# Attention scores as 64-row products of two heads at once, with a head pair and a query tile as the unit of work

## The reference, cut to what matters

```python
k = keys @ Wk.T + bk;  gk = key_grid @ Wgk.T + bgk        # 256 + 256 keys
v = values @ Wv.T + bv; gv = key_grid @ Wgv.T + bgv
q = (queries @ Wq.T + bq)                                 # of the layer-normalised x
att = einsum('bhqd,bhdk->bhqk', q, k_new) / 8             # 16 heads, 64 long
att_k = where(attention_mask, -inf, att[..., :256])       # first 256 keys only
att = softmax(concat([att_k, att[..., 256:]]))
out = einsum('bhqk,bhkd->bhqd', att, v_new) @ Wo.T + bo
x = x + out
x = x + fp8_gemm(layernorm(x), ffn_kernel) + ffn_bias
```

## Time and profile before

| | before |
|---|---|
| median of 3 runs | 2909.78 us (2906.48 to 2913.43) |
| span of the profiled execution | 2906.8 us |
| PE busy | 2793.8 us, 96% |
| PE weight loads busy | 2431.0 us, 84% |
| DVE busy | 2315.1 us, 80% |
| ACT busy | 1982.3 us, 68% |
| POOL busy | 2099.0 us, 72% |
| mean granted TensorE clock | 0.995 of full |

### The profile page before, as it was taken

One profiled execution on the slowest core, in us unless ns is written; L12 is line 12 of the kernel. 1 busy time (PEld: TensorE's weight loads), 2 busy tenths in 40 slices (PEclk: granted clock), 3 DMA queues, 4 the chain that ended last, 5 costly groups with the idle time before them and its releaser, 6 DMA issues.

```text
span 2906.8 us, 68146 instructions
## 1 busy us (share of the span) xinstructions
PE 2793.8 (96%) x20352; PEld 2431.0 (84%) x20352; DVE 2315.1 (80%) x3793; ACT 1982.3 (68%) x4742; POOL 2099.0 (72%) x2504
## 2 busy tenths in 40 slices
PE   5999999999999999999999999999999999999997
PEld 4888888888888888888888888888888888888886
DVE  5888778888778887788887788877888877888776
ACT  4666676766677666767666776667676667766674
POOL 4777777777768777777777687777777776877775
PEclk9999999999999999999999999999999999999998
DMA  5333333333333333333343333333333433333331
GB/s 170 82 77 90 76 86 82 80 79 91 72 90 87 76 90 76 87 83 79 79 92 71 90 87 76 90 77 86 85 79 78 93 69 90 87 76 90 78 82 37
DMA packets 176029, 243.02 MB, mean 84 GB/s; under 512 B 25472, under 2 KB 92544, under 8 KB 176000
## 3 DMA queue, kind: packets, MB, share of 16 engines
q1 hardware_dynamic: 176000, 242.66, 35.6%
HBM read 66.40 MB, written 8.39 MB: 26 GB/s over the span
## 4 chain that ended last, share of the span: by engine, by line
PE 61%; DVE 17%; issue 13%; ACT 7%; DMA 1%; DVEq 1%; POOL 0%; SPq 0%; ACTq 0%; POOLq 0%
PE ps_misc L555 20%; PE ps_o L658 10%; PE ps_pt L645 10%; PE ps_misc L599 8%; PE ps_scores L631 5%; PE ps_scores L632 5%; DVE pt_lo L941 5%; DVE kv_out L912 3%; PE ps_scores L634 2%; ACT probs L786 2%; DVE q_lo L889 2%; DVE scr_b L875 1%; DVE o_t L949 1%; ACT zq_out L751 1%; DVE scr_a L877 1%
## 5 line engine op out<-in xcount | busy, mean ns | idle before, releaser
L481 POOL TENSOR_SCALAR probs<-probs,recips 128x512 f32<-128x512 f32 x1024 | 698.4, 694 | 457.0 <-DVE recips L936 456.8
L795 ACT CAST pt_hi<-ps_pt 128x512 fp32r<-128x512 f32 x1024 | 551.7, 595 | 319.8 <-PE ps_pt L645 314.5
L786 ACT ACTIVATE probs<-ps_scores,neg_max 128x512 f32<-128x512 f32 x1024 | 696.0, 688 | 23.5 <-DVE neg_max L932 11.4
L941 DVE TENSOR_TENSOR pt_lo<-ps_pt,pt_hi 128x512 fp32r<-128x512 f32 x1024 | 655.2, 680 | 53.2 <-ACT pt_hi L795 50.3
L932 DVE TENSOR_REDUCE neg_max<-ps_scores 128x2 f32<-128x1024 f32 x512 | 621.1, 1213 | 9.5 <-PE ps_scores L634 9.5
L658 PE MATMUL ps_o<-pt_hi,v_hl 128*128 128x256 f32 x2048 | 554.6, 302 | 1.0 <-DVE o_t L949 1.0
L645 PE MATMUL ps_pt<-ident,probs 128*128 128x128 f32 x4096 | 531.5, 273 | 1.6 <-DVE pt_lo L941 1.6
L658 PE MATMUL ps_o<-pt_lo,v_hl 128*128 128x256 f32 x2048 | 511.4, 281 | 0.0
L645 PEld LDWEIGHTS ps_pt<-ident,probs 128*128 128x128 f32 x4096 | 464.5, 141 | 8.6 <-POOL probs L481 2.0
L631 PE MATMUL ps_scores<-k_hl,q_hh 128*128 128x512 f32 x1024 | 456.8, 446 | 9.0 <-issue 4.7
L632 PE MATMUL ps_scores<-k_hl,q_lo 128*128 128x512 f32 x1024 | 407.1, 398 | 0.0
(11 more groups left out here) (106 smaller groups left out, 6567.1 us busy)
## 6 DMA issues: line engine op xcount, KB each, us to landing
k_hl<-k_split SPq DMA_DIRECT2D x1024, 128.0 KB, 2.3
mask_sb<-mask_dram SPq DMA_DIRECT2D x128, 256.0 KB, 3.3
q_hh<-q_hh SPq DMA_DIRECT2D x256, 128.0 KB, 2.4
x_sb<-x_dram SPq DMA_DIRECT2D x32, 256.0 KB, 2.8
side_raw<-side_t_dram SPq DMA_DIRECT2D x32, 256.0 KB, 3.6
scr_b<-ctx_t_dram SPq DMA_DIRECT2D x32, 256.0 KB, 2.8
out_dram<-y SPq DMA_DIRECT2D x32, 256.0 KB, 2.1
probs<-wq_t_dram SPq DMA_DIRECT2D x1, 1024.0 KB, 5.1
```

The source lines that it names most:

```text
L481: nc.gpsimd.tensor_scalar(probs[:, h % 2, t, :], probs[:, h % 2, t, :], recips[:, h % 2, t:t + 1], 1.0, ALU.mult, ALU.mult).then_inc(norm_ ...
L786: nc.scalar.activation(probs[:, h % 2, t, :], ps_scores[:, h % 2, t, :], ACT.Exp, bias=neg_max[:, h % 2, t:t + 1], scale=-1.0, accum_out=s ...
L795: nc.scalar.copy(pt_hi[:, h % 2, 2 * k:2 * k + 2, :], ps_pt[:, k, :, :]).then_inc(pthi_done, 1)
L941: V.tensor_tensor(pt_lo[:, h % 2, 2 * k:2 * k + 2, :], ps_pt[:, k, :, :], pt_hi[:, h % 2, 2 * k:2 * k + 2, :].bitcast(F32), ALU.subtract). ...
```

## The change

**Scores.** q and k are kept where the chunk leaves them: `q_hi`, `q_lo`, `k_hi`, `k_lo` hold two heads, one on partitions 0 to 63, the other on 64 to 127. Each of the three products hi·hi, lo·hi, hi·lo is issued with 64 rows, for the first head on the upper half of the array's rows and right behind it for the second head on the lower half; they go to different PSUM banks. The program gives these products an array position of row 0 or row 64 and a size of 64 by 128; all others have position 0 and 128 by 128. The two mask products follow with 128 rows, as before.

**Unit of work.** A unit u is a head pair and one query tile (`pair, t = u // 2, u % 2`). It has as many scores, exponentials, transposes and casts as a head had; the two entries of `ps_scores`, `probs` and `ps_pt` are now two heads of one tile instead of two tiles of one head (in `ps_pt`: instead of two halves of the keys). A head's output product needs both units of its pair. `outputs` of head h-2 now stands ahead of `transposes` of unit h, and `pt_hi` and `pt_lo` have three buffers instead of two.

**Removed.** `k_split`, `place_keys`, `place_queries`, their semaphores and waits, the zeroing of half of `q_lo`, and `B_EARLY`. The split of q is one operation on 128 partitions on each of ACT and DVE instead of two on 64. GpSimd writes k_hi and k_lo directly to their place.

**Chunks.** `PLACES` has the same chunks at other places; in the opening part k1 comes ahead of v0.

Of the diff, cut to its core:

```diff
 PLACES = {
-    (0, "A"): ("k0", 1), (0, "B"): ("q", 1), (1, "A"): ("wo0_prev", 0), (1, "B"): ("k1", 1),
+    (0, "A"): ("k0", 1), (0, "B"): ("q", 1), (1, "A"): ("k1", 1), (2, "A"): ("wo0_prev", 0), (2, "B"): ("v0", 1),
...
-B_EARLY = (1, 2)
...
+def pt_turn(pair, e):
+    return 0 if e == 0 else 1 + pair % 2
...
-            hh = q_hh[:, n % 2].rearrange("p (a e) s -> p e a s", e=2)
-            ql = q_lo[:, n % 2].rearrange("p (a e) s -> p e a s", e=2)
-            src = zq_out[:].rearrange("p (a s) -> p a s", s=S)
-            owns = [slice(e * DK, (e + 1) * DK) for e in range(2)]
-            return [(hh[own, e], ql[own, e], src[own]) for e, own in enumerate(owns)]
+            flat = "p a s -> p (a s)"
+            return [(q_hi[:, n % 2].rearrange(flat), q_lo[:, n % 2].rearrange(flat), zq_out[:])]
...
-                        sp.dma_start(k_hl[to, n % 2, 2 * int(kind[1]) + e, :].bitcast(F32),
-                                     k_split[own, part, :].bitcast(F32)).then_inc(k_placed, 16)
...
-                    sp.dma_start(hh[other, e], hh[own, e]).then_inc(q_placed, 16)
...
-            def scores(h, g, free=True):
+            def scores(u, g, free=True):
+                pair, t = u // 2, u % 2
+                r, a = pair // 2 % 2, pair % 2
+                rows = slice(t * P, (t + 1) * P)
+                if free:
+                    pe.wait_ge(exp_done, 2 * (g - 1))
+                for n, (q, k) in enumerate(((q_hi, k_hi), (q_lo, k_hi), (q_hi, k_lo))):
+                    for e in range(2):
+                        own = slice(e * DK, (e + 1) * DK)
+                        mm(ps_scores[:, u % 2, e, :], q[own, r, a, rows], k[own, r, a, :],
+                           start=(n == 0), stop=False)
+                for e in range(2):
+                    row = (2 * a + e) * QT + t
+                    m = mask_sb[:, r, row * S:(row + 1) * S].bitcast(FP8E5)
+                    last = mm(ps_scores[:, u % 2, e, 0:S], mask_weight[:], m, start=False, stop=True)
+                last.then_inc(scores_done, 1)
+
+            def transposes(u, g, first=False):
+                for e in range(2):
+                    pe.wait_ge(norm_done, 2 * g + e + 1)
+                    if not first:
+                        pe.wait_ge(ptlo_done, 2 * g - 1 + e)
...
+            def outputs(h, g, first=False):
+                pair, e = h // 2, h % 2
+                pe.wait_ge(ptlo_done, 2 * g + (2 if e else 3))
...
                     do((h, "A"))
+                    if not (first and h < 2):
...
+                        outputs((h - 2) % H, g - 2, first and h == 2)
                     transposes(h, g, first and h == 0)
...
+                    do((h, "B"))
```

More of the change, by code:

```diff
@@ L83, in kept @@
             return False
-        return not (last and (kind == "zt_next" or place[0] > LAST_OWN))
+        own = kind in PREV or group > 0
+        return own or not last
     return {place: PLACES[place] for place in SLOT_ORDER if place in PLACES and kept(place, PLACES[place])}
@@ L384, in batch @@
             def batch(b, first=False, last=False):
-                c = Chunks(b, first, last)
                 for h in range(H):
@@ L408, in batch @@
                         load_mask(b + 1, 0)
-                    for place in ((h, "A"), (h, "B")):
-                        kind, n = c.at.get(place, ("", 0))
-                        if kind in K_KINDS:
-                            place_keys(kind, n, c.before(place, KV) + 1)
-                        if kind == "q":
-                            place_queries(n, c.before(place, ZQ) + 1)
             batch(0, first=True)
@@ L470, in split_chunk @@
                 wait_apart(pool, "pool", misc_free, copied)
-                if kind in K_KINDS and not (isinstance(k_before, int) and k_before == 0):
-                    wait_apart(pool, "pool", k_placed, K_PLACES * k_before)
                 nc.gpsimd.tensor_scalar(hi, src, 1.0, 0.0, ALU.mult, ALU.add).then_inc(kv_hi_part, 1)
@@ L503, in _ @@
             for j, (kind, n) in enumerate(PROLOGUE[2:]):
-                split_chunk(kind, n, j + 3, j, sum(k in K_KINDS for k, _ in PROLOGUE[2:2 + j]))
+                split_chunk(kind, n, j + 3, j)
             def batch(b, first=False, last=False):
@@ L519, in batch @@
                         norm(h + 1, H * b + h + 1)
-                    if h == 3 and not first:
+                    if h == 4 and not first:
                         rstd_of(0, mv_y, var_y, rstd_y, b)
@@ L524, in batch @@
                         copy_x(b)
-                    if h == 4 and not first:
+                    if h == 5 and not first:
                         scale_quant_in(b - 1)
@@ L637, in transposes @@
-            def transposes(h, g, first=False):
-                pe.wait_ge(norm_done, QT * (g + 1))
-                for k in range(2):
-                    if not first:
-                        pe.wait_ge(ptlo_done, 2 * g - 1 + k)
-                    for j in range(2):
-                        for t in range(QT):
-                            kt = 2 * k + j
-                            last = nc.tensor.transpose(ps_pt[:, k, j, t * P:(t + 1) * P],
-                                                       probs[:, h % 2, t, kt * P:(kt + 1) * P], ident[:])
-                    last.then_inc(pt_full, 1)
@@ L649, in outputs @@
-            def outputs(h, g, first=False, tiles=range(KT)):
-                if 0 in tiles:
-                    pe.wait_ge(ptlo_done, 2 * (g + 1))
-                    if not first:
-                        pe.wait_ge(o_done, g)
-                n, i = h // GH, h % GH
-                for kt in tiles:
+            def scores(u, g, free=True):
[14 more added lines that the diff above has]
+                last.then_inc(scores_done, 1)
@@ L657, in outputs @@
+            def outputs(h, g, first=False):
+                pair, e = h // 2, h % 2
+                pe.wait_ge(ptlo_done, 2 * g + (2 if e else 3))
+                if not first:
+                    pe.wait_ge(o_done, g)
+                n, i = h // GH, h % GH
+                for kt in range(KT):
                     for pt in (pt_hi, pt_lo):
-                        last = mm(ps_o[:, 0:S], v_hl[:, n % 2, kt, i, :], pt[:, h % 2, kt, :],
+                        last = mm(ps_o[:, 0:S], v_hl[:, n % 2, kt, i, :], pt[:, pt_turn(pair, e), kt, :],
@@ L727, in _ @@
             batch(B - 1, last=True)
+            outputs(H - 2, H * B - 2)
             outputs(H - 1, H * B - 1)
@@ L1047, in batch @@
                         quantise_weights(h - 4)
-                    if h in (5, 6) and not first:
-                        quantise(b, h - 5)
+                    if h in (6, 7) and not first:
+                        quantise(b, h - 6)
                     if h == 7 and not last:
```

185 lines of the change are left out of this document (71 added, 114 removed), and 10 rows, old and new, of the table PLACES.

## The result

The changed kernel takes 3012.98 us (median of 4 runs, 3009.55 to 3014.7) against 2908.53 of the kernel before: a ratio of 1.0356, with a 95% interval of 1.0341 to 1.0371. It is 104 us slower. 2850 us were forecast, with a range of 2790 to 3050: the result lies inside the range, but on the other side of the kernel before.

The account below looks back on a forecast made before the run. TensorE was taken as the bound, hardly ever kept waiting. Scores gave 59 us less, everything else 0: 2906.8 - 59 = 2848, plus 3 from span to median, 2851, rounded 2850 us; own range 2820 to 2895, full range 2790 to 3050.

Parts of the forecast that it names:

- What bounds the kernel: Whole kernel before: TensorE is hardly ever kept waiting, so the time is the sum of distances between its starts.
- The scores, after: Scores of a unit: three pairs side by side, lag, two masks and entry sum to 1.075 us; 59 us less in all.
- I take the middle, 0.04: Entry to a unit's first 64-row product: 0.04 us, between 0 and 0.08 seen at changes of kind on the full array.
- The lag of 0.10: Scores: the second product of each pair starts one load behind the first, seen once a unit, 0.10 us.
- its 1.19: Scores of a head before the change: 1.19 us, over 512 heads 609 us, 21% of the span.
- Rival 1: Scores block edges: every array-size change runs the array dry, up to 0.16 us each; 3035, half price 2970; chance 0.24.
- rival 3: Scores pairs: a half's weights can't load while it streams, so further pairs take 0.335 instead of 0.235; 2953; chance 0.09.
- So no new wait: 0: Outputs and transposes: only their order changes, and the split of the transposes stays covered; 0, or 16 us if cover fails.
- the prediction's own sign: Scores block in the profile after: if the time moves and its length doesn't, the prediction's whole reasoning is wrong.
- Copies and splits: DMA copies and q splits on ACT and DVE: copies were hidden, worth 0 to 3 us; splits 0.

Follow-up runs that it names:

- e6_before_late: The kernel before, with the statistics, scaling and quantisation of y one step later and xq_prev at (8, B) instead of (7, B): 2960.5 us (1.0175).
- e3_one_half: The changed kernel with both products of every pair on rows 0 to 63, so the two can't run side by side: 3253.6 us (1.1184).
- e5_mask_between: The changed kernel with xq_prev at (9, A) instead of (8, B) and both masks moved between the first and second pair: 3143.6 us (1.0813).
- e18_fine2: The changed kernel with other places, y's quantisation two operations each in steps 5 to 7, next x's statistics and normalisation one step later: 2910.3 us (1.0009).
- e7_two_units: The changed kernel with xq_prev at (9, A) and both units' scores of a head pair in one block every odd step: 3407.8 us (1.1749).

## Why the prediction was wrong

**What bounds the kernel**: right for the kernel before, and too quickly carried over. TensorE was the bound only as long as DVE's results just arrived. e6_before_late shows how close that was: one step later costs 52 us.

**The scores, after**: the halves do run together (0.23 from pair to pair; e3_one_half costs 241 us more). The terms mis-sized were the edges. "I take the middle, 0.04" for the entry is 0.09, the exit, for which I had nothing, is 0.10, and in the block shown the masks take 0.28 instead of 0.23 (ahead of outputs the median is 0.23). The lag of 0.10 has the right size by luck: no second product starts a load behind the first (0.49 alone, 0.50 for both); it is the load of the first pair, which nothing hides behind a change of size, so it is a part of the edge. The row became 12 us shorter at full clock, not 59: 47 us of the miss. The reasoning by the nearest rows, changes of kind on the full array, had no change of size among them, and the middle between 0 and 0.08 was no estimate of it. The sum also took its 1.19 from a block behind outputs, where one between two chunks has 1.27.

**Rival 1** had the place, ahead of the first 64-row product and of the first mask; measured is about 0.1 an edge (0.28 for two edges and the load in e5_mask_between). That takes the gain but, at +4 us over all blocks, is no loss. Its direction came true, but for the most part by waits that it did not name, and its 2970 for half the price doesn't follow from the sum, which gives 1.235 to 1.275 us a unit and so 2933 to 2953. The Trainium skill's page "TensorEngine Tiling (Array Packing)", Key Properties, says that a change of mode drains TensorE; the trace agrees in so far as each way in and out costs 0.28 us. On rival 3 the trace disagrees with Part 3 of the Trainium skill's "TensorE: Matmul & The Clock Gate": third pairs follow 0.23 behind second ones, and their loads begin as the second pair does (1405.89), so loads run beside products of the same half.

**Outputs, transposes and chunks: "So no new wait: 0"** is the step that failed. It covers 115 of the 163 us by which I missed: 81 of idle time and 34 of half clock behind it. By the prediction's own sign (the time moves, the block's length doesn't) it was wrong in its whole reasoning; that 3013 us lies in its range is owed to the width that rivals 1 and 3 gave it. I followed one chain (`pt_lo`) and k's way over GpSimd, and not the third that the new table touches: `ps_misc` is freed by DVE behind `pt_lo`, and where v stands at B and another chunk at A of the next step, only a block of scores lies between. Nor did I see that `normalise_y`, the quantisation and xq moved by a step while the moments and the normalisation of the next x stayed, which puts them side by side on DVE. The kernel before already showed this as its longest wait, `ps_misc` behind `kv_out`. The runs show it as a matter of places: with other places and smaller pieces (e18_fine2) most of the idle time (115 us, against 99 before) and all of the additional half clock (0.995) are gone, and the scores are the same.

**Copies and splits**: right, they were hidden. The splits gave DVE and ACT time back that neither needed; q_lo takes 894 ns on 128 partitions, between my 0.69 and 1.65 (zt_lo, which gave the 1.65, has 0.82 in the changed kernel):
```profile
L847 DVE TENSOR_TENSOR q_lo<-zq_out,q_hi 128x512 fp32r<-128x512 f32 x128 | 114.5, 894 | 73.1 <-ACT q_hi L736 73.1
```

What stays open: how much of the 52 us of e6_before_late is the place of xq and how much the rest of the shift; what the new order of outputs and transposes costs by itself, which no run separates from the places; how far the kernel before could be tuned in the same way; and whether fewer changes of size would pay, since the one arrangement tried (e7_two_units) broke the chain behind the scores.

## What to carry to other kernels

Two half-height products side by side take the time of one, but here each way into and out of the half-height size cost 0.28 us; so count what lies between two changes. Three pairs in place of four full-height products save 0.235 us, which was too little to gain. When a rewrite comes with a new order, price the order by itself: follow each buffer with one copy (here `ps_misc`) to the engine that frees it, and to what stands ahead of that copy in its queue. An engine that is 73% busy can hold one that is 94% busy if its work comes in lumps.

## What the runs showed of the hardware

- Products of 64 rows on different halves of the array, into different PSUM banks, run together at the pace of one: 0.23 us for a pair of 512 columns, with a load for each (e3_one_half: 0.46 for two on the same half). The two start within 0.01 us, and their loads within 0.01 too (two loads in 0.19 us).
- A change from 128 rows to 64 delays the next product by 0.09, the change back by 0.10. Behind the change to 64 rows the first product's weight load isn't hidden, another 0.10, with a partner or without one (e3_one_half). Together 0.28 us (e5_mask_between: 142 us for 512).
- Idle gaps of TensorE of 1.10 and 0.98 us, 2.6 us apart, came ahead of a fall to 1.2 GHz (mean granted clock 0.66 over 5 us); 73 us more at that level cost about 34 us in all. In e6_before_late, which has the wait for xq but none for `o_t` behind it, the mean clock stayed at 0.995.
